# Batched router block, a second output slab and two weight slots in an attention and FFN kernel

## What is computed

```python
xn = layernorm(x)
q = xn @ Wq.T + bq; k = xn @ Wk.T + bk; v = xn @ Wv.T + bv      # 32 heads, 16 kv heads, 128 wide
s = softmax(causal(q @ k.T / sqrt(32))) @ v
base   = xn @ base_W.T
probs  = softmax(xn @ router_W.T)                               # 8 experts
w      = one_hot(top_2(probs)) * top_vals / sum(top_vals)
mid    = (xn @ lora_A) * w                                      # 8 experts x rank 16 = 128 columns
g      = silu(base + 2 * mid @ lora_B)
out    = x + s * g
```

## Time and profile before

| | us |
|---|---|
| median of 2 runs | 2441.38 (2367.28 and 2515.47) |
| profiled execution | 2368.29 |
| its span (slowest core, core 3) | 2366.7 |
| spans of the 8 cores | 2349.9 to 2366.7 |
| stage A | 0 to 342 |
| stage B, Q and K | 342 to 1001 |
| stage B, router and V | 1001 to 1307 |
| stage C | 1307 to 1824 |
| stage D | 1824 to the end |

### The profile page before, as it was taken

How to read it: one execution, slowest core, us unless ns; L and a number is a source line. 1 busy time by engine, 2 the same in 40 slices (tenths; PEclk the granted TensorE clock), 3 DMA queues, 4 the chain that set the end, 5 groups by cost and what they waited for, 6 DMA issues and landing times.

```text
span 2366.7 us, 33093 instructions; the slowest of 8 cores (2349.9 to 2366.7 us)
## 1 busy us (share of the span) xinstructions
PE 1857.4 (78%) x12788; PEld 1163.6 (49%) x12788; DVE 339.2 (14%) x1047; ACT 552.4 (23%) x677; POOL 93.6 (4%) x92
## 2 busy tenths in 40 slices
PE   1064339999999999998799599999998547575773
PEld 0011014444444444466587288888887224343442
DVE  0002670000000000003100000000000445333222
ACT  0054000110101011000100011111110548586882
POOL 0011000000000000000000000000000000000000
PEclk7588559999999999999899799999999669898997
DMA  9999005455555444263050434444431455535224
GB/s 161 162 157 128 0 5 54 56 54 59 58 61 62 54 56 54 41 80 44 19 80 18 50 58 75 72 75 78 75 65 51 123 117 146 107 114 116 61 79 86
DMA packets 231002, 177.99 MB, mean 75 GB/s; under 512 B 123587, under 2 KB 219076, under 8 KB 226372
## 3 DMA queue, kind: packets, MB, share of 16 engines
q0 software_dynamic: 155408, 85.53, 31.9%
q1 hardware_dynamic: 73140, 73.57, 12.2%
q10 hardware_dynamic: 2304, 16.78, 2.1%
HBM read 194.27 MB, written 67.11 MB: 110 GB/s over the span
## 4 chain that ended last, share of the span: by engine, by line
PE 64%; DMA 9%; DVE 9%; ACT 7%; another core or an unknown queue 4%; issue 4%; SPq 1%; DVEq 0%; POOL 0%; ACTq 0%; POOLq 0%
PE psB L344 9%; PE psA L344 9%; PE pg L344 9%; ACT arena L754 7%; PE pg L553 6%; PE psA L553 6%; PE psB L553 6%; DMA arena<-xT 5%; PE psA L474 3%; PE pg L474 3%; PE psB L474 3%; DMA out<-arena 3%; PE pav L661 2%; DVE arena L302 2%
## 5 line engine op out<-in xcount | busy, mean ns | idle before, releaser
L344 PE MATMUL pg<-arena,wstr 128*128 128x512 bf16 x1024 | 237.6, 388 | 68.5 <-DVE arena L302 68.5
L344 PE MATMUL psA<-arena,wstr 128*128 128x512 bf16 x1024 | 223.6, 379 | 0.0
L344 PE MATMUL psB<-arena,wstr 128*128 128x512 bf16 x1024 | 223.6, 379 | 0.0
L754 ACT ACTIVATE arena<-psB,konst 128x1024 bf16<-128x1024 f32 x160 | 178.3, 1114 | 114.7 <-PE psB L747 113.1
L344 PEld LDWEIGHTS pg<-arena,wstr 128*128 128x128 bf16 x1024 | 101.0, 99 | 203.8 <-issue 88.2
L754 ACT ACTIVATE arena<-psA,konst 128x1024 bf16<-128x1024 f32 x160 | 178.1, 1113 | 31.8 <-PE psA L747 28.1
L553 PE MATMUL pg<-wstr,arena 128*128 128x256 bf16 x1408 | 162.2, 275 | 24.9 <-DMA wstr<-bwT 24.9
L661 PE MATMUL pav<-vsb,arena 128*128 128x129 bf16 x960 | 81.3, 235 | 114.2 <-DVE arena L767 114.1
L553 PEld LDWEIGHTS pg<-wstr,arena 128*128 128x128 bf16 x1408 | 138.9, 99 | 42.6 <-issue 25.4
L344 PEld LDWEIGHTS psA<-arena,wstr 128*128 128x128 bf16 x1024 | 100.2, 98 | 120.8
L344 PEld LDWEIGHTS psB<-arena,wstr 128*128 128x128 bf16 x1024 | 100.2, 98 | 120.8
(11 more groups left out here) (111 smaller groups left out, 1418.5 us busy)
## 6 DMA issues: line engine op xcount, KB each, us to landing
arena<-xT POOLq DMA_DIRECT2D x32, 512.0 KB, 12.3
wstr<-wqT POOLq DMA_DIRECT2D x16, 1024.0 KB, 17.7
wstr<-bwT POOLq DMA_DIRECT2D x8, 2048.0 KB, 20.3
gH<-vsb SPq DMA_DIRECT2D x128, 128.0 KB, 1.8
arena<-gH ACTq DMA_DIRECT2D x16, 1024.0 KB, 5.7
out<-arena POOLq DMA_DIRECT2D x16, 1024.0 KB, 15.8
Qs<-vsb SPq DMA_DIRECT2D x64, 128.0 KB, 2.5
wstr<-wkT POOLq DMA_DIRECT2D x8, 1024.0 KB, 15.1
```

Of the source, the lines that this page charges most:

```text
L344: em.emit("T", lambda E, pp=pp, sl=sl, ch=ch, ts=ts: nc.tensor.matmul(pp[:, :], wbuf[sl][:, ch * 128:(ch + 1) * 128], xnT[:, ch * T + ts * ...
L754: nc.scalar.activation(wT[wsl][:, kc0 * 512: kc0 * 512 + 1024], ps[:, 0:1024], AF.Exp, bias=konst[:, 0:1], scale=SCALE),
```

## The change

It has four parts. (1) `keep` and `lmsk` grow from 8 to 128 columns, and the 16 rounds of `piece_rtrans` become one round of the same twelve operations on all 128 columns; the per-group values are handed in as views that repeat each value 8 times (`b8`). (2) The four `mid` slices use the banks `pg0`, `pg1`, `psAa`, `psAb` instead of `pg0` and `pg1` in turn, while `MGT` is still the pair of counts of `pg0` and `pg1`; and of the base FFN's groups only the first of the first two blocks waits for `MGT`. (3) The slab becomes two, `s_slab`, used in turn by block, and a scaling waits for the output DMA of the block before last. (4) To make room, `wT` has two slots instead of three, the `g` slots move, and the Q and K slots move to `wstr`; the first Q loads wait in addition for the FFN to be finished (`CBM_W`). The multiplication by `g` waits for `dofq` as before.

The waits of the first score matmul of a unit (`("dav", wav[wsl])`) are unchanged in text, but `wsl` is now `qh_ctr % 2`.

```diff
@@ -127,8 +127,8 @@
         nm2 = en(nc.sbuf_tensor("nm2", [128, 16], F32))
         trow = en(nc.sbuf_tensor("trow", [128, 16], F32))
         inv2 = en(nc.sbuf_tensor("inv2", [128, 16], F32))
-        keep = en(nc.sbuf_tensor("keep", [128, 8], F32))
-        lmsk = en(nc.sbuf_tensor("lmsk", [128, 8], F32))
+        keep = en(nc.sbuf_tensor("keep", [128, 128], F32))
+        lmsk = en(nc.sbuf_tensor("lmsk", [128, 128], F32))
         recip = en(nc.sbuf_tensor("recip", [128, 4], F32))
 
         arena32 = arena.bitcast(F32)
@@ -136,13 +136,12 @@
         vsb32 = vsb.bitcast(F32)
 
         xnT = arena
-        s_sb = arena32[:, 0:8192]
-        g_slot = [arena32[:, 8192 + 2048 * i: 8192 + 2048 * (i + 1)]
+        s_slab = [arena32[:, 0:8192], arena32[:, 8192:16384]]
+        g_slot = [arena32[:, 16384 + 2048 * i: 16384 + 2048 * (i + 1)]
                   for i in range(4)]
-        wT = [arena[:, 32768:40960], arena[:, 40960:49152],
-              arena[:, 55296:63488]]
-        q_slot = [arena[:, 49152 + 512 * i: 49152 + 512 * (i + 1)] for i in range(4)]
-        k_slot = [arena[:, 51200:53248], arena[:, 53248:55296]]
+        wT = [arena[:, 49152:57344], arena[:, 57344:65536]]
+        q_slot = [wstr[:, 4096 + 512 * i: 4096 + 512 * (i + 1)] for i in range(4)]
+        k_slot = [wstr[:, 0:2048], wstr[:, 2048:4096]]
 
         mrow = wstr32[0:1, 4096:6144]
         qrow = wstr32[0:1, 6144:8192]
@@ -387,48 +386,54 @@
                 em.emit("V", lambda E: nc.vector.tensor_copy(
                     lgn[:, :], pg[0][:, 0:128]),
                     waits=[("ctg", 16)], inc=("f_pg0", 1))
-                for tc in range(16):
-                    sl8 = lgn[:, tc * 8:(tc + 1) * 8]
-                    w = [("f_pg0", em.c("f_pg0"))] if tc == 0 else []
-                    em.emit("V", lambda E, sl8=sl8, tc=tc: nc.vector.reduce_max(
-                        nm1[:, tc:tc + 1], sl8, AX.X, negate=True),
-                        waits=w, inc=("ct", 1))
-                    em.emit("V", lambda E, sl8=sl8, tc=tc: nc.vector.tensor_scalar(
-                        sl8, sl8, nm1[:, tc:tc + 1], None, ALU.add),
-                        waits=[("ct", em.c("ct"))], inc=("ct", 1))
...
-                    em.emit("V", lambda E, tc=tc: nc.vector.tensor_scalar(
-                        wd_sb[:, tc * 8:(tc + 1) * 8], keep[:, :], inv2[:, tc:tc + 1],
-                        None, ALU.mult),
-                        waits=[("ct", em.c("ct"))], inc=("cw", 1))
+                def b8(ap2d, stride):
+                    return bass.AP(ap2d.tensor, ap2d.offset,
+                                   [[stride, 128], [1, 16], [0, 8]])
+                lgn3 = lgn.rearrange("p (g n) -> p g n", n=8)
+                e3 = e_sb.rearrange("p (g n) -> p g n", n=8)
+                keep3 = keep.rearrange("p (g n) -> p g n", n=8)
+                wd3 = wd_sb.rearrange("p (g n) -> p g n", n=8)
+                lmsk3 = lmsk.rearrange("p (g n) -> p g n", n=8)
+                nm1b = b8(nm1[:, :], 16)
+                trowb = b8(trow[:, :], 16)
+                inv2b = b8(inv2[:, :], 16)
+                em.emit("V", lambda E: nc.vector.reduce_max(
+                    nm1[:, :], lgn3, AX.X, negate=True),
+                    waits=[("f_pg0", em.c("f_pg0"))], inc=("ct", 1))
+                em.emit("V", lambda E: nc.vector.tensor_tensor(
+                    lgn3, lgn3, nm1b, ALU.add),
+                    waits=[("ct", em.c("ct"))], inc=("ct", 1))
+                em.emit("V", lambda E: nc.vector.tensor_scalar(
+                    keep[:, :], lgn[:, :], 0.0, None, ALU.is_ge),
+                    waits=[("ct", em.c("ct"))], inc=("ct", 1))
+                em.emit("V", lambda E: nc.vector.scalar_tensor_tensor(
+                    lmsk[:, :], keep[:, :], -1e30, lgn[:, :], ALU.mult, ALU.add),
+                    waits=[("ct", em.c("ct"))], inc=("ct", 1))
...
+                em.emit("V", lambda E: nc.vector.tensor_tensor(
+                    keep3, e3, trowb, ALU.is_ge),
+                    waits=[("ct", em.c("ct"))], inc=("ct", 1))
+                em.emit("V", lambda E: nc.vector.tensor_mul(
+                    keep[:, :], keep[:, :], e_sb[:, :]),
+                    waits=[("ct", em.c("ct"))], inc=("ct", 1))
+                em.emit("V", lambda E: nc.vector.tensor_tensor(
+                    wd3, keep3, inv2b, ALU.mult),
+                    waits=[("ct", em.c("ct"))], inc=("cw", 16))
+
             def piece_wdtrans():
                 for half in range(2):
                     pname = "pg%d" % half
@@ -512,9 +517,7 @@
 
 
             for ts in range(4):
-                psl = ts % 2
-                pname = "pg%d" % psl
-                pp = pg[psl]
+                pp, pname = bcb[ts % 6]
                 aq = acquire(pname)
                 w = [("cld", CLD), aq]
                 for ch in range(NCH):
@@ -548,7 +551,9 @@
                     gi = ob * 16 + tc
                     pp, pname = bcb[gi % 6]
                     aq = acquire(pname)
-                    w = [("cb%d" % sl, 16 * bld[sl]), aq] + list(MGT)
+                    w = [("cb%d" % sl, 16 * bld[sl]), aq]
+                    if ob < 2 and tc == 0:
+                        w += list(MGT)
                     for ch in range(NCH):
                         em.emit("T", lambda E, pp=pp, sl=sl, ch=ch, tc=tc: nc.tensor.matmul(
                             pp[:, 0:256], xnT[:, ch * T + tc * 128: ch * T + tc * 128 + 128],
@@ -610,7 +615,7 @@
                     w.append(("dqf%d" % qsl, quse[qsl]))
                 elif qsx == 0:
                     w += [("f_qkst0", 16 * use.get("qkst0", 0)),
-                          ("f_qkst1", 16 * use.get("qkst1", 0))]
+                          ("f_qkst1", 16 * use.get("qkst1", 0))] + CBM_W
                 quse[qsl] += 1
                 em.emit("Y", lambda E, qidx=qidx, qsl=qsl, qsx=qsx: E.dma_start(
                     q_slot[qsl][:, :], Qs[qidx, :, qsx * 512:qsx * 512 + 512]),
@@ -671,14 +676,14 @@
                     recip[:, qc:qc + 1], pt[:, 128:129]),
                     waits=[("dav", DAV), ("dvc", em.c("dvc")), aq],
                     inc=("dvc", 1))
-                em.emit("V", lambda E, pt=pt, qc=qc, qidx=cx["qidx"]:
+                em.emit("V", lambda E, pt=pt, qc=qc, qidx=cx["qidx"], qs=qs:
                         nc.vector.tensor_scalar(
-                            s_sb[:, qc * 2048 + qidx * 128:
-                                 qc * 2048 + qidx * 128 + 128],
+                            s_slab[qs % 2][:, qc * 2048 + qidx * 128:
+                                           qc * 2048 + qidx * 128 + 128],
                             pt[:, 0:128], recip[:, qc:qc + 1],
                             None, ALU.mult),
                         waits=[("dvc", em.c("dvc")),
-                               ("dofq%d" % qc, 16 * qs)],
+                               ("dofq%d" % qc, 16 * max(0, qs - 1))],
                         inc=("f_" + pname, 1))
 
             kuse = {0: 0, 1: 0}
@@ -686,7 +691,7 @@
             batch_ctr = 0
             qh_ctr = 0
             pexp = {0: 0, 1: 0}
-            wav = {0: 0, 1: 0, 2: 0}
+            wav = {0: 0, 1: 0}
             xg_use = {0: 0, 1: 0}
             out_ct = 0
             def emit_vload(qsx):
@@ -714,7 +719,7 @@
                         qidx = j * 8 + i
                         qsl, dq_w = qld_cnt[(qs, u)]
                         _, dk_w = kld_cnt[(qs, i)]
-                        wsl = qh_ctr % 3
+                        wsl = qh_ctr % 2
                         nb = kmax // 2
                         seq = []
                         pos = {}
@@ -792,12 +797,12 @@
                     w = SEV + [("dg%d" % qc, 16 * (qs + 1)),
                                ("dofq%d" % qc, 16 * qs),
                                ("dfin", em.c("dfin"))]
-                    em.emit("V", lambda E, qc=qc: nc.vector.tensor_mul(
-                        s_sb[:, qc * 2048:(qc + 1) * 2048],
-                        s_sb[:, qc * 2048:(qc + 1) * 2048], g_slot[qc][:, :]),
+                    em.emit("V", lambda E, qc=qc, qs=qs: nc.vector.tensor_mul(
+                        s_slab[qs % 2][:, qc * 2048:(qc + 1) * 2048],
+                        s_slab[qs % 2][:, qc * 2048:(qc + 1) * 2048], g_slot[qc][:, :]),
                         waits=w, inc=("dfin", 1))
-                    em.emit("P", lambda E, qc=qc, r0=r0: E.dma_start(
-                        out[r0:r0 + 128, :], s_sb[:, qc * 2048:(qc + 1) * 2048],
+                    em.emit("P", lambda E, qc=qc, r0=r0, qs=qs: E.dma_start(
+                        out[r0:r0 + 128, :], s_slab[qs % 2][:, qc * 2048:(qc + 1) * 2048],
                         accum_op=ALU.add),
                         waits=[("dfin", em.c("dfin")), ("dpre", 64)],
                         inc=("dofq%d" % qc, 16))
```

44 lines of the change are left out of this document (15 added, 29 removed).

## The result

The changed kernel takes 2296.48 us in the median of nine runs. The kernel before, measured beside it, took 2414.72 us in the median of eight. The ratio of the two is 0.970, with a 95% interval of 0.968 to 0.972, so the change makes the kernel 3.0% faster. (Some executions of either kernel showed a disturbed die; both medians hold such executions, and the ratio leaves them out.) The forecast was 2285.2 us, 3.5% under the profiled execution of before, in a range of 2271 to 2305. The direction was right and the time lies in the range, but of the 83.1 us of the sum only 68.4 arrived in the profile: the profiled execution after has a span of 2298.3 us against 2366.7.

The account below looks back on a forecast made before the run. TensorE was taken to bound the projection stages, and in attention, with no engine full, a loop through three engines; 29.6 + 13.8 + 42.7 - 3.0 = 83.1 us off the profiled 2368.29 gave 2285.2 us, range 2271 to 2305.

Parts of the forecast that it names:

- Router block: V projection: with 16 rounds made one, TensorE's idle time behind ScalarE's queue and its slow restart go; 29.6 us gained.
- `MGT`: Start of the base FFN: the load of `bwT` is released two mid slices sooner; 13.8 us gained, 11.2 to 16.4.
- The slab's masks: Attention block boundaries: masks come 37.5 us sooner in sum, plus 5.2 us of clock recovery; 42.7 us gained.
- Two weight slots at nothing: Attention units: the score matmul's new wait ends when the pair would start anyway; cost 0, upper bound 18 us.
- Rival B: Attention units: the third weight slot was cover, each of 64 units pays 0.28 us; 2303.2 us, chance 0.08.
- The clock in the long stages: Projection stages: TensorE's granted clock was taken to stay at 1.00, not to fall once its pauses are gone.
- Rival D: Long projection stages: without pauses TensorE is granted a lower clock, making the kernel slower; 2416 us, chance 0.03.
- C: Attention stage: output traffic and loads hold all three boundaries as long as the slab did; 2324.9 us, chance 0.06.
- The K and Q loads: First attention boundary: loads beside the output DMA land late, 3 us lost, bounds 0 and 8; nothing at later boundaries.
- Rival A: First attention boundary: K and Q loads starve until the output is written; loss 8 us, 2290.2 us, chance 0.10.
- half speed: Loads beside the output DMA: by packet turns a small load lands in about 6 us, on time; 3 us less lost.

Follow-up runs that it names:

- mgt4: The changed kernel with `MGT` extended to the four banks of the mid slices, so `bwT` is again released after slice 3: 2304.38 us, ratio 0.976 to the kernel before.
- wt3: The changed kernel with the third weight slot given back in the free part of `wstr`: 2289.15 us, ratio 0.968 to the kernel before.
- oneslab: The changed kernel with both slab names on the same memory and the old wait for the output DMA: 2318.66 us, ratio 0.983 to the kernel before.
- ahead: The changed kernel with four K and eight Q slots, loads issued four units earlier: 2273.7 us, ratio 0.961 to the kernel before.

## Why the forecast was right, and where it was not

**Router block: right.** Forecast 29.6, measured 28.0 in the stretch and 31.5 when taken back. The round took 4.5 us, inside the bound of 3.1 to 7, and hid completely. VectorE's operations on 128 values cost 0.23 to 0.29 us each. The 1.6 us short are the one group at the lower clock (5.33 us for 3.67), which the sum did not have; cores 1 and 3, which run it in 3.67, have 29.4 and 29.7 us less in the stretch.

**`MGT`: right.** The load was released one pair of slices sooner, as read from the counts. It was issued 1.25 us after the multiplication, as before, but TensorE started 25.7 us after the issue against 23.6 before (1293.22 to 1318.89; 1335.78 to 1359.34). That took 2.1 us; a group 1.0 us shorter gave some back, and the total is 12.7 us. Neither is the change's doing: the first of the two loads lands after 19.8 to 25.1 us before, on the eight cores, and after 20.7 to 25.7 now, and in mgt4, where it again runs after the mid matmuls, it took 24.6 (1302.17 to 1326.83). Between two such cores 2 us are scatter. The mean over the cores, 13.5 us less idle time and no change in the group behind it, is what the term of 13.8 said, with the low clock staying as taken.

**The slab's masks: right.** Forecast 37.5 us for the masks and 5.2 for the clock. Measured, the three distances over the boundary shrank from 21.34, 21.63 and 22.85 to 6.36, 8.86 and 12.41, together by 38.2. The periods behind them shrank from 6.95, 8.93 and 12.01 to 4.98, 7.58 and 9.72, together by 5.6. That is 43.8 for 42.7.

**Two weight slots at nothing: right.** The periods of the steady loops are 4.98, 7.34 and 9.7, and wt3 gained nothing clear of its interval. The score pair still waits 0.28 us for the group of the unit before, as in the earlier trace rows. Rival B falls.

**The clock in the long stages: right.** Over 420 to 1060 us the granted clock is 1.00 after as before, and so it is over 1330 to 1780 us, in the FFN. Rival D falls, and so does C: it needed late loads of 12 us three times, and there are 11.9, 4.4 and none.

**The K and Q loads: wrong, and this is the step that failed.** The step read "bounds 0 and 8; I take 3 us lost", and "at the later boundaries [...] I take nothing there". The period with the late load was 16.89 instead of 4.98 us, 11.9 lost, and at the second boundary 11.76 instead of 7.34, 4.4 lost: 16.3 for 3.0. (10.81 us of the 11.9 are the wait itself, the rest is the unit behind it, with score pairs of 1.01 us for 0.59.) With that term the sum is 28.0 + 12.7 + 43.8 - 16.3 = 68.2, against the 68.4 of the spans (in the rest some smaller terms of either sign, +1.8 to -1.9 us, cancel). How large the term is depends on the core and the execution: in the second profile the slowest core loses 9.2 us at the first boundary and 0.25 at the second. On every one of the sixteen cores profiled the first wait is over the 3 us taken, and on ten of them over 8, the upper bound. Rival A had the mechanism, with a chance of 0.10 and a price of 8; it was the true case, and dearer. That the time still lies in the range is luck as far as this step goes: its bounds were 0 to 8, and the room came from rival B at 2303.2 and from low ends of the other terms, none of which happened. Three things in the step failed.

First, the value in the bound. I went by the `gH` store beside `bwT`, most of which landed in 1.8 us, although the case at hand was another: a load beside four megabytes of output in flight. The other end of the bound, a load that lands once the output is through, is what happened: output through at 1902.9, Q landed at 1903.6.

Second, the bound itself took the end of the output from before. There nothing else was moving at the time: the K load at 1942.97 was issued after the output had landed. Now K and two Qs, half a megabyte, are moved among the 4 MB of the output. An eighth of 27.5 us is 3.4, and 4.1 us is what the output got longer, 2.6 in the mean over the cores. The runs bear this out in part: in oneslab, where the loads come after the output, it takes 27.3 us on core 7 as before the change, and in ahead, where one K and two Q loads run beside it, 29.5.

Third, "the loads have 10 us and more" at the second boundary compared the slack with the 3.2 us of a free transfer. K was 11.8 us and Q 13.0 us under way there. At the third boundary the units are 9.7 us, and there indeed nothing waits.

The sentences on the Trainium skill (*DMA: Bandwidth & Descriptors*, "Queues, rings and completion order") said that by its rule of turns, packet by packet, the load goes at half speed and lands in about 6 us. The counts agree with turns: 30 packets to 25, and 94 to 82. "Half speed" was my step and was wrong. An output row carries four times the bytes of a K row; beside it the loads moved 25 packets in 2 us where alone they moved 374. (The profile counts every row of 8, 2 or 1 KB as a packet. A packet of that section is several descriptors, and how many rows one turn takes no run here shows.) What the rule leaves out is the first 4 us in which no packet of the load appears, under either size of output packet.

**What stays open.** Why the first packet comes about 4 us after the issue while the output runs (alone it came after 0.9 to 1.4 us). It wasn't tried by itself. How much of the output's extra time is the loads' is known only from the comparison of oneslab, ahead and the changed kernel above. Why the wait at the second boundary is 4.5 us on one core and 0.6 on another. Also why in all kernels with this order of emission one unit each of blocks 1 and 3 is 0.4 to 0.65 us longer than its neighbours; it is under 2 us in all.

## What to carry to other kernels

When a change removes a stall, ask what was in flight during the stall and is now beside the restarted work: the first transfer that the restarted work needs has to be priced with that traffic, and the nearest row for it is the end of the traffic, not the free transfer. A load with a lead of two short units is safe only as long as nothing large is being written; four more units of lead cost 12 KB of slots a partition here and were worth 17 us (some 7 of them in block 0, where nothing is written), while cutting the big transfer's packets was worth nothing. And small dependent operations belong in one batch even when their engine is nearly idle, as their price (27 us here) is paid by whoever is queued behind them.

## What the runs showed of the hardware that I had not expected

- A load of 256 KB that lands in about 3 us alone takes 14.9 us beside an accumulating output DMA of 4 MB, and its first packet appears some 4 us after the issue. It does no harm where the load has the lead: with four more units of it the loads took 13.1 and 15.3 us beside the same output and nobody waited.
- Two DMA queues with work moved about the same number of packets at either size of the output's: 30 to 25 at 8 KB against 2 KB and smaller, 94 to 82 at 2 KB. A threefold packet rate for the small load made no difference to the time, 0.973 for 0.970.
- The lower clock behind a pause cost TensorE 1.3 to 2.5 us in the next 32 matmuls (5.00 to 6.20 us for 3.67), and the length of the pause doesn't show in it: 5.00 to 6.13 us after pauses of 22 to 27 us before the change, 5.10 to 6.20 after pauses of 9 to 14 us with it. And a group of 32 that follows two lone matmuls with 0.7 and 0.2 us of idle time ran 1.66 us longer on four of eight cores with the change, on six in the second profile and on none before, and what tells these cores from the others I did not find.
- VectorE's `scalar_tensor_tensor` on 128x128 values in f32, one operand from PSUM and one from SBUF, takes 351 ns, the same as the scaling by a reciprocal that it replaced.
